# Fewer row-sum matmuls in one causal attention: pairs of key tiles added on VectorE first

## What is computed

```python
H, D = 16, 32
q = jnp.einsum('bsc,hcd->bhsd', xn, wq)
k = jnp.einsum('btc,hcd->bhtd', yn, wk)
v = jnp.einsum('btc,hcd->bhtd', yn, wv)
a = jax.nn.softmax(jnp.einsum('bhsd,bhtd->bhst', q, k) * D ** (-0.5), axis=-1)
mask = (jnp.arange(t)[None, :] > jnp.arange(s)[:, None])   # keeps keys AFTER the query
a = a * mask
o = jnp.einsum('bhst,bhtd->bhsd', a, v)
```

## Time and profile before

| | us |
|---|---|
| median of 3 runs | 3260.39 |
| lowest, highest | 3251.67, 3262.79 |
| the profiled execution: its own time | 3268.76 |
| the profiled execution: its span | 3267.0 |
| PE busy | 2732.1 (84%) |
| DVE busy | 1909.6 (58%) |
| ACT busy | 1469.3 (45%) |
| POOL busy | 1078.9 (33%) |

### The profile page before, as it was taken

How to read it: one execution, slowest core, us unless ns; L and a number is a source line. 1 busy time by engine, 2 the same in 40 slices (tenths; PEclk the granted TensorE clock), 3 DMA queues, 4 the chain that set the end, 5 groups by cost and what they waited for, 6 DMA issues and landing times. The chain is left out here.

```text
span 3267.0 us, 45506 instructions
## 1 busy us (share of the span) xinstructions
PE 2732.1 (84%) x17204; PEld 1570.5 (48%) x17204; DVE 1909.6 (58%) x3481; ACT 1469.3 (45%) x1978; POOL 1078.9 (33%) x980
## 2 busy tenths in 40 slices
PE   5888888869879899998878898898998996788544
PEld 3443433623345444445743444587787875333222
DVE  4655655667756544444666666644544433766688
ACT  2556556236732354455325555534333331466322
POOL 3223332223220255565217777620010111022333
PEclk7999997879989899999889999899999998789666
DMA  7566562055520011112000000002211212555000
GB/s 171 114 117 140 122 123 64 1 116 123 123 94 14 17 38 41 47 44 73 27 14 1 1 1 14 13 13 64 81 58 56 66 51 81 96 111 101 26 10 15
DMA packets 130376, 202.76 MB, mean 62 GB/s; under 512 B 36368, under 2 KB 66608, under 8 KB 129520
## 3 DMA queue, kind: packets, MB, share of 16 engines
q1 hardware_dynamic: 98416, 147.46, 19.5%
q0 software_dynamic: 31744, 52.41, 5.9%
HBM read 134.92 MB, written 64.78 MB: 61 GB/s over the span
## 5 line engine op out<-in xcount | busy, mean ns | idle before, releaser
L2383 DVE TENSOR_REDUCE L_mx<-bank_t 128x2 f32<-128x1024 f32 (+3 forms) x512 | 565.2, 1121 | 335.9 <-PE bank_t L2189 213.8
L2383 DVE TENSOR_REDUCE L2a_mx<-bank_t 128x2 f32<-128x1024 f32 x256 | 311.9, 1223 | 348.8 <-PE bank_t L2166 347.8
L2586 ACT ACTIVATE L_P<-bank_t 128x1024 f32<-128x1024 f32 (+3 forms) x384 | 340.3, 916 | 262.2 <-PE bank_t L2201 144.0
L2586 ACT ACTIVATE L2a_P<-bank_t 128x1024 f32<-128x1024 f32 x256 | 261.8, 1024 | 257.9 <-PE bank_t L2178 257.4
L2189 PE MATMUL bank_t<-L_KS,L_QS 48*128 48x512 f32 (+2 forms) x1024 | 243.2, 478 | 123.9 <-ACT L_P L2586 48.6
L2166 PE MATMUL bank_t<-L2a_QK 32*128 32x512 f32 x1536 | 253.9, 439 | 53.6 <-ACT L2a_P L2586 25.5
L2201 PE MATMUL bank_t<-L_QS,L_KS 50*128 50x512 f32 (+2 forms) x1024 | 244.9, 482 | 21.2 <-DVE L_mx L2383 12.6
L2174 PE MATMUL bank_t<-L2a_QK 32*128 32x512 f32 x1536 | 255.2, 443 | 0.0
L2166 PEld LDWEIGHTS bank_t<-L2a_QK 32*128 32x128 f32 x1536 | 136.9, 192 | 217.0 <-ACT L2a_P L2586 119.1
L2201 PEld LDWEIGHTS bank_t<-L_QS,L_KS 50*128 50x128 f32 x1024 | 101.2, 198 | 260.3 <-issue 174.6
L2231 PE MATMUL bank_o<-L_P,L_V 128*32 128x512 f32 (+3 forms) x1536 | 205.7, 612 | 8.8 <-ACT L_P L2586 6.1
(11 more groups left out here) (455 smaller groups left out, 5997.9 us busy)
## 6 DMA issues: line engine op xcount, KB each, us to landing
L_KS<-L_spill_k_halves SPq DMA_DIRECT2D x174, 128.0 KB, 5.6
L_QS<-L_spill_q_halves SPq DMA_DIRECT2D x174, 128.0 KB, 4.6
L_spill_raw<-xn POOLq DMA_DIRECT2D x64, 256.0 KB, 2.5
L2g_raw<-in_L_ffn_h_blocks SPq DMA_DIRECT2D x32, 512.0 KB, 3.8
L_spill_k_halves<-L_hi SPq DMA_DIRECT2D x32, 256.0 KB, 2.1
L_spill_k_halves<-L_lo SPq DMA_DIRECT2D x32, 256.0 KB, 2.4
L_spill_q_halves<-L_hi SPq DMA_DIRECT2D x32, 256.0 KB, 2.7
L_spill_q_halves<-L_lo SPq DMA_DIRECT2D x32, 256.0 KB, 3.1
```

Of the source, the lines that this page charges most:

```text
L2383: e.tensor_reduce(neg, s.tile[:, :, 0:n_keys], AX.X, ALU.max, negate=True).then_inc(sem(s.done), 1)
L2586: e.activation(s.at.Pr[s.pb][:, :, q0:S], s.tile[:, :, q0:S], ACT.Exp, scale=s.at.scale).then_inc(sem(s.exp), 1)
```

## The change

- The key tiles go in the order 0, 1, 2, 3 in all modes.
- `P` has 7 buffers here rather than 6.
- The ones matmul is issued at two of the four key tiles only: at tile 2 with its own `P` (opening the sum), and at tile 3 with the `P` of tile 0 (closing it). Before that, VectorE adds the `P` of tile 1 and then that of tile 3 onto the `P` of tile 0 (new step `AddPair`, 128 x 1024 fp32, in place). Each add is delayed to the tick after its tile's exp; in the last tick of all it isn't delayed. It waits for the exp and for the mask copy of tile 0; the V block of tile 3 waits for it.
- A chore runs in a tick only if that tick's V block is of tile 0 or 1 ("light"), or if more than three chores wait. Before, it ran in any tick.

```diff
-            NP_ = 7 if pooled else 6
+            NP_ = 7 if D == 32 else 6
...
-                return [3, 2, 1, 0] if mode == "upper" else [0, 1, 2, 3]
+                return [0, 1, 2, 3]
...
+            ADDED, ALONE = {1: "vector", 3: "vector"}, (2,)
+
+            def add_pair(first, part, by):
+                done = due("pair_added_" + by)
+                dst, src = at.Pr[first[0]][:, :, :], at.Pr[part[0]][:, :, :]
+                add(AddPair(dst, src, by, [part[1], first[1], first[3], pair_added.get(first[0])], done))
+                P_free[part[0]] = P_free[part[0]] + [done]
+                pair_added[first[0]] = done
...
+                sums_of, e_sum = None, None
+                if upper and place in ALONE:
+                    sums_of = parts[0][0], place == ALONE[0], False
+                elif upper and last:
+                    sums_of, e_sum = (head[0], False, True), pair_added.pop(head[0])
+                add(Values(at, un, g, kt, first, last, parts, i_v, sums_of,
+                           [e_v, *[p[1] for p in parts], *[p[3] for p in parts], o_free[0] if first else None, e_sum], mm))
...
                             def other_work(p=p):
+                                light = True
                                 if len(pending) > lag:
-                                    pending.pop(0)()
+                                    values_of, light = pending.pop(0)
+                                    values_of()
                                 if at_tick == prep_at:
                                     queue_up(new)
-                                run_due(chore=any_tick or p == at.GP - 1 or (pooled and len(chores) > 2))
+                                run_due(chore=(light or len(chores) > 3) if upper else any_tick or p == at.GP - 1 or (pooled and len(chores) > 2))
...
+                            elif upper and place == 0:
+                                head = parts[0]
+                            elif upper and place in ADDED:
+                                pair = lambda head=head, part=parts[0], by=ADDED[place]: add_pair(head, part, by)
+                                if at_tick == len(flat) - 1:
+                                    pair()
+                                else:
+                                    delayed.append((tick[0], pair))
...
-                            if s.at.GP == 1 and i == 0:
-                                mm = e.matmul(bank_o[row + 32:row + 64, :], ones[:, 0:32], s.at.Pr[pb][:, c, :],
-                                              start=s.first, stop=s.last, tile_position=(0, row + 32))
+                            if s.summed is not None and i == 0:
+                                whole, opens, closes = s.summed
+                                mm = e.matmul(bank_o[row + 32:row + 64, :], ones[:, 0:32], s.at.Pr[whole][:, c, :],
+                                              start=opens, stop=closes, tile_position=(0, row + 32))
...
+                elif kind is AddPair and s.by == "vector":
+                    dve.wait_ge(*s.after)
+                    e.tensor_tensor(s.dst, s.dst, s.src, ALU.add).then_inc(sem(s.done), 1)
```

More of the change, by code:

```diff
@@ L101 @@
 Logits = namedtuple("Logits", "at un s kt tile after mm pb exp_after exp")
-Values = namedtuple("Values", "at un g kt first last parts i_v after mm")
+Values = namedtuple("Values", "at un g kt first last parts i_v summed after mm")
+AddPair = namedtuple("AddPair", "dst src by after done")
 CopyGroup = namedtuple("CopyGroup", "at un g raw after done raw_dram den_dram out_after landing")
@@ L509, in attention @@
             sums_free, inv_free, summed, n_sums = [None] * 4, [None, None], {}, [0]
-            n_pair, n_group, n_diag = [0], [0], [0]
+            n_pair, n_group, n_diag, pair_added = [0], [0], [0], {}
             tick, delayed, chores, maxima, last_chore = [0], [], [], [], [-9]
@@ L727, in scale, with values @@
                 last_unit(un)
-            def values(un, g, kt, place, parts):
+            def values(un, g, kt, place, parts, head=None):
                 i_v, e_v, n_v_tiles = v_ready[un.b, un.j]
@@ L733, in values @@
                 first, last = place == 0, place == TB - 1
-                add(Values(at, un, g, kt, first, last, parts, i_v, [e_v, *[p[1] for p in parts], *[p[3] for p in parts],
-                                                                    o_free[0] if first else None], mm))
+                sums_of, e_sum = None, None
[5 more added lines that the diff above has]
+                           [e_v, *[p[1] for p in parts], *[p[3] for p in parts], o_free[0] if first else None, e_sum], mm))
+                if e_sum is not None:
+                    P_free[head[0]] = P_free[head[0]] + [mm]
                 for pb, _, i_d, _ in parts:
@@ L875, in attention @@
                            [[step] for step in entry.side.rest()] + entry.later_steps()]
-            pending, at_tick = [], 0
+            pending, at_tick, head = [], 0, None
             for un in units:
@@ L906, in attention @@
                                     un, p, place, part)))
+                            elif upper and place == 0:
[6 more added lines that the diff above has]
+                                    delayed.append((tick[0], pair))
                             at_tick += 1
-                        pending.append(lambda un=un, g=g, kt=kt, place=place, parts=parts: values(
-                            un, g, kt, place, parts))
+                        pending.append((lambda un=un, g=g, kt=kt, place=place, parts=parts, head=head: values(
+                            un, g, kt, place, parts, head), place in (0, 1)))
                 finished.add(un.n)
@@ L912, in attention @@
             while pending:
-                pending.pop(0)()
+                pending.pop(0)[0]()
             if following is None:
```

## The result

| | before | changed | ratio, 95% interval |
|---|---|---|---|
| median, first series (13 runs each) | 3251.67 | 3241.04 | 0.9959 [0.9943, 0.9975] |
| median, second series (18 and 12 runs) | 3257.63 | 3248.16 | 0.9970 [0.9954, 0.9987] |
| the profiled execution: its span | 3267.0 | 3229.7 | |
| PE busy | 2732.1 | 2687.4 (83%) | |
| DVE busy | 1909.6 | 1985.5 (61%) | |

The changed kernel is 3 to 4 parts in a thousand faster, that is 9.5 to 13 us. The prediction said 15.4 us less and a median of 3245.0; the range and the sign hold.

A forecast was written before the change was run, and what follows sets the result against it. PE bounds ticks with a chore, the PE-DVE loop of 2.36 us those without. Gains of 25.1 less 1.7, 3.7 and 4.3 give 15.4 us less, from a median of 3260.4 to 3245.0; range 3229 to 3264.

The forecast's parts named there:

- the law of a tick: Each tick lasts the longer of 2.36 us (loop PE to DVE and back) and 1.13 + V + chore (PE).
- tick 0, tile 1: Nine projections beside the shorter V block of tile 1 in tick 0 save 0.42 us each, 3.8 us.
- tick 3, tile 0: Eleven projections beside the shorter V block of tile 0 in tick 3 save 0.64 us each, 7.0 us.
- tick 7, tile 0: Thirteen projections beside the shorter V block of tile 0 in tick 7 save 0.64 us each, 8.3 us.
- turnings: Tick 4, with the turning of maxima, falls from 2.72 to the loop's 2.36 us, saving 14 x 0.36 = 5.0 us.
- early transposes: Three early transposes, of the same kind as the turnings, save 1.0 us.
- an add ahead of a maximum: After tick 4, an add delays the next maximum by 0.15 us in 11 units or so, costing 1.7 us.
- an add behind POOL's low half: In tick 4, the add waits for POOL and the next maximum starts 0.74 late; five units, 3.7 us.
- end of the stage: Adds hold up DVE's last statistics and PE waits at its first turn; 4.3 us later, bounds 0 and 8.
- The lock: DVE instructions with two SBUF inputs and POOL instructions keep each other waiting; without this the sum would be 3.7 us better.
- rival 2: POOL's mask copies go first, adds wait 0.73 more; net 2 us less, 3258, no measurable change; chance 0.22.
- rival 3: TensorE's clock falls in the stage, S and V taking 4.26 us at the low level; 15 us slower, 3275; chance 0.08.

The follow-up runs named there:

- experiment 9: The changed kernel with ones at all four tiles and no adds in units 14 and 15, and the first group's tile 3 add one tick later; median 3233.83, ratio 0.9933.
- Experiment 8: The changed kernel with each add issued twice in a row on DVE; the middle of the stage took 329.0 us against 295.6.
- experiment 3: The changed kernel without its 64 adds, ones still at two tiles; the stage took 381.1 us against 391.1.
- experiment 4: The changed kernel with ones at all four tiles and no adds in unit 15; median 3239.41, ratio 0.9955.
- experiment 5: The changed kernel with ones at all four tiles and no adds in units 14 and 15; median 3234.95, ratio 0.9932.
- experiment 6: The changed kernel with ones at all four tiles and no adds in unit 14 alone; the end of the stage took 42.7 us.
- experiment 7: The changed kernel with seven unused fp32 matmuls of 512 columns on PE ahead of the first turn; the end took 45.7 us instead of 48.5.
- experiment 11: The changed kernel with units 14 and 15 plain (all ones, no adds) and the tile 3 add one tick later in six places; median 3238.14, ratio 0.9943.

## Why the prediction was nearly right

The code was read right, and so was the law of a tick. Against the kernel with the rule alone, term by term:

| step | predicted | measured |
|---|---|---|
| tick 0, tile 1 | 9 x 0.42 = 3.8 | 9 x 0.44 = 4.0 (4.05 to 3.61) |
| tick 3, tile 0 | 11 x 0.64 = 7.0 | 11 x 0.65 = 7.2 (4.07 to 3.42) |
| tick 7, tile 0 | 13 x 0.64 = 8.3 | 13 x 0.65 = 8.5 (4.07 to 3.42, 5.81 to 5.16) |
| turnings | 14 x 0.36 = 5.0 | 13 x 0.36 = 4.7; unit 14 only 0.05 |
| early transposes | 1.0 | 2 x 0.38 = 0.8 |
| an add ahead of a maximum | 11 x 0.15 = 1.7 | 0 (2.37 with, 2.37 without) |
| an add behind POOL's low half | 5 x 0.74 = 3.7 | 6 x 0.49 = 2.9 |
| end of the stage | 4.3, at most 8 | 11.1 |

- **The gain** was right in place, count and size. The distances of 0.14 and 0.11 us between short matmuls gave V blocks of 0.36 and 0.58 us; the ticks give 0.35 and 0.56.
- **The exposed add** cost nothing. I let it start when the maximum ends, at 2.25 us into the tick. The rows of experiment 9 show it starting 0.08 us before the maximum ahead has ended (1219.17 + 1.23 = 1220.40 against 1220.32), as a DVE instruction with nothing to wait for does in these traces. So it ends at 3.38 instead of 3.47 us, just when the next scores are there (2.37 + 1.01). Experiment 8 shows that this is a fit and not slack.
- **The lock** was right as a mechanism and a third too dear. The add ends 3.94 us into the tick (1213.79 less 1209.85) as against 4.08, and the maximum behind it starts 0.07 us before that end, at 3.87, where it would start at 3.38 without a delay: 0.49 instead of 0.74. I also missed one place, tick 1 of unit 13. The rule in the Trainium skill, SBUF — State Buffer, § Who interferes with whom, agrees with these rows: an add that meets the low half ends 1.07 us after it, an add's 1.22 less some overlap, and so do all 17 such adds of the stage. Experiment 9 takes the meeting away and the time comes back.
- **The race with the mask copies** (rival 2) went the way of the forecast nearly everywhere: the copies start after the adds, mostly by 0.1 to 0.3 us, and are the ones that wait, mean 1109 ns against 743, inside their slack. In three places of the middle (tick 0 of units 6, 10 and 14) an add came second and took 1.47 us, and its tick was no longer for it. It decided nothing.
- **The end of the stage** is the step that failed: 11.1 us instead of 4.3. I had the right event, statistics held up by the adds and PE waiting at its first turn. I took them to start 4.5 us later and had them ahead of PE's need by 2 us; but of the two adds one waits for POOL's bias addition (2.38 us) and takes 2.83, the reciprocal comes 1.2 us later, and PE comes 2.5 us sooner. So the wait is 6.8 us, and the late tick 6.6 longer than before. What I left out altogether is what happens to the clock in that place: ticks of 4.05, 3.87 and 3.87 us where before they took 3.38, 2.12 and 2.12, which is 4.2 us (and 3.87 where rival 3 had reckoned with 4.26). The last tick is 2.1 longer, at the low clock and with an add ahead of the last V block, and the lighter V blocks of the ticks before give 1.8 back: 11.1. Of these 11.1 us 6.9 go with the adds and 4.2 are there without any (experiment 3). I had the clock as a rival for the whole stage (rival 3), where it stayed at 1.00, and not as a price of the one wait that I predicted.

The errors partly cancel: the exposed adds and the lock cost 2.5 us less than I said, the end 6.8 more; that leaves a gain of some 11 us by the terms. The stage shows 9.4, and its first unit accounts for most of the difference: it took 26.9 us against 25.8 with the rule alone. There the low clock lasted longer in this execution, and ticks 4 and 5 took 4.05 and 3.87 us as against 2.72 and 2.39.

That the median of 3245.0 came so close (3241.04) is luck in a second way: it was counted from a median before of 3260.4, of three runs, and that of the thirteen is 3251.67. From there the same 15.4 us would have given 3236.3. It is the drop that tests the prediction, 15.4 against 9.5 to 13 us.

## What to carry to other kernels

Work taken off an engine pays only in those ticks in which that engine is the longest; here half of the ones matmuls gave 18 us in the middle out of 63 busy ones, and only with the other work moved into these ticks. An addition that is put into a queue is free as long as what stands behind it isn't wanted sooner, so look at the last units on their own: their queues hold the next stage's first steps, and here the additions cost 6.9 us in the last two units and 3.0 in all before. An engine made faster just ahead of such a step only waits for it longer. And where you predict that TensorE will wait, price the clock after the wait as well.

## What the runs showed of the hardware

- DVE instructions in a row overlap by 0.08 us where the second has nothing to wait for (1219.17 + 1.23 against 1220.32), so an add that the list gives as 1.22 us takes 1.14 in a chain. Without this the exposed additions would have cost some 0.09 us each, by the sum above.
- Waits of 1.6 to 1.7 us before a turn went with a low clock for 10 to 17 us behind them (a wait of 6.8 us with 23.9 us), in which a tick of 2.12 us takes 3.87. In ticks of the middle waits of 1.32 us were followed by a low clock in three cases and not in five, so the wait is not all that counts.
- Executions differ in the first 50 us of the stage as well, in kernels whose steps there are nearly the same (the changed one and experiments 3 to 7, 9 and 11), and more so the longer the clock stays low: units 0 and 1 took 45.2 us with 16 us at the low clock, 46.9 to 47.0 with 17 to 22, and 50.7 with 30.
